# Cross-attention of 16 sequences: a prologue reordered, its work moved among the first heads, and values six heads behind

## Chip, core and metric

One NeuronCore of a Trainium2 chip runs the whole kernel. The metric is the device time of one execution in microseconds (us).

## What is computed

```python
mu = jnp.mean(input, axis=(1, 2), keepdims=True)
var = jnp.var(input, axis=(1, 2), keepdims=True)
xn = (input - mu) * jax.lax.rsqrt(var + EPS)
xn = xn * gamma[None, :, None] + beta[None, :, None]
q = jnp.einsum('oc,ncs->nos', Wq, xn) + bq[None, :, None]
kv = jnp.einsum('od,nds->nos', Wkv, context) + bkv[None, :, None]
q = q.reshape(n, h, c, s).transpose(0, 1, 3, 2)
kv = kv.reshape(n, 2 * h, c, -1).transpose(0, 1, 3, 2)
k, v = (kv[:, :h], kv[:, h:])
att = jax.nn.softmax(jnp.einsum('nhqc,nhkc->nhqk', q * scale, k * scale), axis=-1)
y = jnp.einsum('nhqk,nhkc->nhqc', att, v)
y = y.transpose(0, 1, 3, 2).reshape(n, h * c, s)
return input + jnp.einsum('co,nos->ncs', Wo, y) + bo[None, :, None]
```

There are 16 sequences of 64 channels and 256 positions, 8 heads of 64 channels, and a context of the same shape as x. All is float32.

## The kernel before

Everything is done per sequence n and head h. The products of weights are made once: A = Wq transposed times Wk for each head (`products_a`, split into a high part in a format that TensorE takes at full speed, `a_hi`, and the rest, `a_lo`), and B = Wv times Wo for each head (`b_sb`, then scaled and split into `b_w`). So a head needs these steps:

- t: A applied to the normalised x, two heads a turn (L383, L384), in a PSUM bank. ScalarE copies the high part (`t_a`, L519), VectorE subtracts it from the bank for the low part (`t_b`, L722). Then the bank is free. In the steady stretch there is one bank, `ps_t`.
- first maxima: one coarse product of `t_a` and the context (L420) into `ps_max` (two banks, one a head); VectorE takes the negative maximum of each row (L738). The maxima of a sequence are transposed on TensorE (L464) into `ps_m`, copied by ScalarE (L545) and brought by a DMA as one more row into `t_b`, so that the scores come out with the maximum taken off.
- scores: `c_seq` with `t_a` and `t_b` (L401, L402) into `ps_sc` (two banks). ScalarE makes the exponential twice, in fp16 (`p_hi`, L527, four buffers) and in fp32 (`p_full`, L529, two buffers), and GpSimd subtracts them (`p_lo`, L609). `p_full` of head h therefore waits for `p_lo` of head h - 2. For the last heads VectorE makes every second `p_lo` (`LO_ON_VECTOR`).
- u: B applied to the context, two products (kt = 0, 1) for each sequence into `ps_m` (L454, L455), split by ScalarE (`u_hi`, L538) and VectorE (`u_lo`, L776).
- values: `p_hi` and `p_lo` times `u_hi` and `u_lo` (L361 to L363), 24 matmuls a pair of heads into `ps_z`, with the sum of the exponentials as one more column. VectorE takes the reciprocal and scales (L733, L745, `z_n`).
- the eight heads are added in three steps (`z_4` on GpSimd L617, `z_2` on VectorE L756, `z_1` on GpSimd L623), transposed on TensorE (L432, "y") into `ps_m`, added to the residual x (L768, `x_res`) and stored.

`ps_m` is one bank for u, the transposed maxima and y, so these follow each other.

Each engine runs the same function `step(n, h)` in order and meets the others at semaphores. `at(n, h, shift)` says which head lies `shift` steps on: t is made 14 heads ahead (`T_AHEAD`), the first maxima 12 ahead (`MAX_AHEAD`), the values of a pair of heads 4 behind. In a step TensorE does: values, t, scores, maxima, y, u, transposed maxima. y lies at h = 1, u at h = 3 and 7, the transposed maxima at h = 5. `run` starts at n = -3, writes sequences up to 1 out, loops over pairs of sequences 2 to 11, and writes the rest out again.

The prologue before the steps loads x in two layouts (`x_res` for the statistics and the residual, `x_raw` for the products), the context and the weights, makes A, the statistics of all sequences (L665, then means across partitions by TensorE, L320 and L324), and the scale and shift of x (L681 to L689). x is then normalised and split: for sequences 0 and 1 on VectorE and ScalarE straight into `x_seq`, for the others by GpSimd (`xn`, L584), ScalarE (high, L499) and VectorE (low, L648) into `x_all`, from which a DMA brings each sequence into `x_seq`. The context is split by GpSimd in four chunks (L571, L573). A bound for u (`tops` over the flat context, L698, and over B, L707) gives the scale of B (L711 to L716), and GpSimd splits B (L590 to L594). GpSimd adds the output bias to all of `x_res` in one instruction (L603).

## Time and profile before

| | us |
|---|---|
| median of 3 runs | 246.66 (246.32 to 248.56) |
| the profiled execution | 246.8 |
| its span in the profile | 245.0 |
| busy: TensorE matmuls | 214.4 |
| busy: VectorE | 214.4 |
| busy: ScalarE | 194.2 |
| busy: GpSimd | 195.6 |

The span is what the profile covers; 1.8 us of the profiled execution lie outside it. Busy times are sums over the span, and a stretch in which an engine is busy all the time can lie beside one in which it waits. In the profile PE is TensorE (PEld its weight loads, which overlap the matmuls), DVE is VectorE, ACT is ScalarE, POOL is GpSimd, SP the engine that issues the DMAs.

### The profile page before, as it was taken

The numbers are of one execution on the slowest core, as the hardware profiler recorded it, in microseconds if no ns is written. First come the engines' busy times: TensorE is split into PE (matmuls) and PEld (weight loads), VectorE is DVE, ScalarE is ACT, GpSimd is POOL, SyncE is SP. The second block draws the span as 40 slices with busy tenths as digits, with TensorE's granted clock in tenths as the row PEclk, the third lists the DMA queues.
The fourth block names the chain that finished last, engine by engine and source line by source line (L and its number), as shares of the span: only waits on it lengthen the run. The fifth ranks groups of instructions, "written<-read, shape, count | busy, mean of one in ns | idle before, by whom it ended". The sixth has DMA issues, their size and how long they took to land.

```text
span 245.0 us, 8138 instructions
## 1 busy us (share of the span) xinstructions
PE 214.4 (87%) x2746; PEld 199.0 (81%) x2746; DVE 214.4 (87%) x447; ACT 194.2 (79%) x391; POOL 195.6 (80%) x188
## 2 busy tenths in 40 slices
PE   0663597799889999999999999999999999998962
PEld 0563476699779999999999999999999999996851
DVE  3288998999997999999999999999999999997684
ACT  2244324999788999999999999999999999999860
POOL 3036995877998998989898989898989999998580
PEclk9999999999999999999999999999999999999996
DMA  6999601121032121212121212121212121010000
GB/s 141 219 284 211 141 3 55 32 58 36 2 89 64 36 68 35 64 33 64 33 64 33 64 33 64 33 64 33 64 33 64 37 64 36 13 33 17 13 0 23
DMA packets 13412, 15.08 MB, mean 62 GB/s; under 512 B 2064, under 2 KB 11920, under 8 KB 13200
## 3 DMA queue, kind: packets, MB, share of 16 engines
q1 hardware_dynamic: 13072, 14.16, 21.9%
q10 hardware_dynamic: 320, 0.66, 1.2%
q8 instruction: 11, 0.18, 0.3%
q14 instruction: 9, 0.07, 0.1%
HBM read 5.90 MB, written 1.05 MB: 28 GB/s over the span
## 4 chain that ended last, share of the span: by engine, by line
PE 64%; DVE 11%; POOL 9%; issue 5%; DMA 4%; ACT 4%; SPq 1%; POOLq 0%
PE ps_max L420 10%; PE ps_sc L401 10%; PE ps_sc L402 10%; POOL p_lo L609 8%; PE ps_t L383 6%; PE ps_z L361 6%; PE ps_z L363 5%; PE ps_z L362 5%; PE ps_t L384 5%; DMA x_res<-x_tiles 4%; PE ps_m L455 3%; PE ps_m L454 3%; DVE neg_max L738 1%; DVE x_seq L648 1%; ACT p_full L529 1%
## 5 line engine op out<-in xcount | busy, mean ns | idle before, releaser
L609 POOL TENSOR_TENSOR p_lo<-p_full,p_hi 128x512 f16<-128x512 f32 x122 | 142.8, 1189 | 23.1 <-ACT p_full L529 23.0
L738 DVE TENSOR_REDUCE neg_max<-ps_max 128x2 f32<-128x512 f32 x128 | 84.4, 663 | 0.0
L529 ACT ACTIVATE p_full<-ps_sc 128x512 f32<-128x512 f32 x128 | 78.4, 613 | 0.5 <-POOL p_lo L609 0.5
L527 ACT ACTIVATE p_hi<-ps_sc 128x512 f16<-128x512 f32 x128 | 77.0, 602 | 1.9 <-PE ps_sc L402 1.8
L401 PE MATMUL ps_sc<-t_a,c_seq 128*128 128x256 f32 x256 | 67.8, 286 | 0.2 <-ACT p_full L529 0.2
L402 PE MATMUL ps_sc<-t_b,c_seq 65*128 65x256 f32 x256 | 67.4, 284 | 0.0
L361 PEld LDWEIGHTS ps_z<-u_hi,p_hi 128*128 128x128 f16 x512 | 46.4, 97 | 13.2 <-issue 10.8
L361 PE MATMUL ps_z<-u_hi,p_hi 128*128 128x65 f16 x512 | 52.9, 194 | 3.2 <-DVE p_lo L783 2.4
L362 PE MATMUL ps_z<-u_lo,p_hi 128*128 128x64 f16 x512 | 52.7, 192 | 0.0
L363 PE MATMUL ps_z<-u_hi,p_lo 128*128 128x65 f16 x512 | 52.7, 193 | 0.0
L519 ACT ACTIVATE t_a<-ps_t 128x512 fp32r<-128x512 f32 x60 | 35.9, 598 | 18.5 <-PE ps_t L384 17.5
L401 PEld LDWEIGHTS ps_sc<-t_a,c_seq 128*128 128x128 f32 x256 | 48.5, 189 | 0.4 <-ACT p_full L529 0.4
L402 PEld LDWEIGHTS ps_sc<-t_b,c_seq 65*128 65x128 f32 x256 | 48.6, 190 | 0.0
L722 DVE TENSOR_TENSOR t_b<-ps_t,t_a 64x512 fp32r<-64x512 f32 x60 | 40.9, 682 | 7.7 <-ACT t_a L519 5.8
L362 PEld LDWEIGHTS ps_z<-u_lo,p_hi 128*128 128x128 f16 x512 | 46.5, 98 | 0.3
L363 PEld LDWEIGHTS ps_z<-u_hi,p_lo 128*128 128x128 f16 x512 | 46.6, 97 | 0.0
L420 PE MATMUL ps_max<-c_max,t_a 128*128 128x256 f32 x224 | 45.1, 282 | 0.0
L383 PE MATMUL ps_t<-x_seq,a_hi 128*128 128x256 f32 x120 | 36.9, 329 | 6.0 <-ACT x_seq L497 3.9
L420 PEld LDWEIGHTS ps_max<-c_max,t_a 128*128 128x128 f32 x224 | 35.1, 191 | 0.0
L384 PE MATMUL ps_t<-x_seq,a_lo 128*128 128x256 f32 x120 | 31.7, 286 | 0.0
L383 PEld LDWEIGHTS ps_t<-x_seq,a_hi 128*128 128x128 f32 x120 | 23.5, 196 | 7.3 <-ACT x_seq L497 3.9
L776 DVE TENSOR_TENSOR u_lo<-ps_m,u_hi 128x512 f16<-128x512 f32 x32 | 22.0, 687 | 5.4 <-ACT u_hi L538 5.4
(101 smaller groups left out, 311.3 us busy)
## 6 DMA issues: line engine op xcount, KB each, us to landing
ctx_raw<-ctx SPq DMA_DIRECT2D x8, 256.0 KB, 17.0
c_seq<-c_all SPq DMA_DIRECT2D x16, 128.0 KB, 2.0
x_seq<-x_all SPq DMA_DIRECT2D x14, 128.0 KB, 2.0
c_max<-c_all SPq DMA_DIRECT2D x14, 128.0 KB, 2.0
x_res<-x_tiles SPq DMA_DIRECT2D x4, 256.0 KB, 7.2
z_n<-ctx_flat SPq DMA_DIRECT2D x1, 1024.0 KB, 14.7
c_seq<-c_all SPq DMA_DIRECT2D x16, 64.0 KB, 2.0
out<-x_res SPq DMA_DIRECT2D x16, 64.0 KB, 1.7
```

The source lines that it names most:

```text
L361: mm(ps_z[:, bank, z0:z0 + Z_W], p_hi[:, buf, kt, qs], u_h, start=(kt == 0), stop=False)
L362: mm(ps_z[:, bank, z0:z0 + C], p_hi[:, buf, kt, qs], u_l, start=False, stop=False)
L363: last = mm(ps_z[:, bank, z0:z0 + Z_W], p_lo[:, buf, kt, qs], u_h, start=False, stop=(kt == KT - 1))
L383: mm(bank[:, k * S:(k + 1) * S], a_hi[:, head + k, :], x_seq[:, q, 0, :], start=True, stop=False)
L384: last = mm(bank[:, k * S:(k + 1) * S], a_lo[:, head + k, :], x_seq[:, q, 1, :], start=False, stop=True)
L401: mm(ps_sc[:, bank, kt * S:(kt + 1) * S], c_seq[:, par, 0, keys], t_a[:, par, head, :], start=True, stop=False)
L402: last = mm(ps_sc[:, bank, kt * S:(kt + 1) * S], c_seq[0:C + 1, par, 1, keys], t_b[0:C + 1, par, head, :], start=False, stop=True)
L420: last = mm(ps_max[:, bank, qt * S:(qt + 1) * S], t_a[:, q, head, qt * P:(qt + 1) * P], c_m, start=True, stop=True)
L527: nc.scalar.activation(p_hi[:, buf, :, :].rearrange("p t s -> p (t s)"), scores, ACT.Exp).then_inc(act_phi, 1)
L529: nc.scalar.activation(p_full[:, head % 2, :], scores, ACT.Exp).then_inc(act_p, 1)
L609: nc.gpsimd.tensor_tensor(p_lo[:, buf, :, :].rearrange("p t s -> p (t s)"), p_full[:, head % 2, :], p_hi[:, buf, :, :].rearrange("p t s -> ...
L738: nc.vector.tensor_reduce(neg_max[:, (par + dn) % 2, head, :], ps_max[:, head % 2, :].rearrange("p (t s) -> p t s", t=KT), X, ALU.max, neg ...
```

## The change

- **Steps.** `run` starts at n = -1, and nothing is looped. Up to step (1, 1) tables say which t turn, which first maxima, which `t_b`, which u and which transposed maxima belong to a step. Of the t turns, the first seven use four banks (`ps_t`, `ps_z` twice, `ps_sc`). The first maxima of sequence 0 follow each other in steps (-1, 1) to (-1, 6), and its four `t_b` come after them at (-1, 7).
- **Prologue.** The DMAs are issued in another order, wk and w on the SP queue; the last two context pieces are loaded from steps (-1, 1) and (-1, 2). TensorE runs 16 products of constants as soon as these are there, and 4 more before t (`keep_warm`); `products_a` and `products_b` go around the statistics' products. ScalarE makes x of sequences 0 and 1 by one activation with scale and bias (`scaled`), and the high parts of the context. The rsqrt refinement is one VectorE instruction shorter. The flat maximum of the context, the bound, the scale and the split of B (now ScalarE and VectorE) and u of sequence 0 come in steps (0, 0) to (0, 5).
- **x for later sequences.** For sequences 2 to 5 GpSimd normalises, for 6 to 15 ScalarE does, one sequence a step (m - 6, 4), with the high part at (m - 6, 6). The low part of every sequence from 2 on is GpSimd's; for m from 6 on at step (m - 5, 3). The low parts of the later context pieces are GpSimd's at (0, 2), (1, 2) and (4, 2), each behind a wait for its own `p_lo`. The output bias is added to `x_res` in four chunks, at (1, 6), (5, 6), (9, 6) and (13, 6).
- **Buffers and order.** `p_hi` and `p_lo` have 8 buffers instead of 4; `p_full` keeps 2. The values of a pair lie 6 steps behind instead of 4. From step (1, 2) on y is at h = 2, the transposed maxima at h = 4, u at h = 5 and 7, and the first u product waits for `act_mt` of its own sequence. `z_4` moves to h = 5, `z_2` to h = 7, `z_1` to h = 0 of the next sequence.

```diff
-T_EARLY = 6
-T_AHEAD, MAX_AHEAD, AV_BEHIND = 14, 12, 3
+T_EARLY = 7
+T_AHEAD, MAX_AHEAD, AV_BEHIND = 14, 12, 5
+P_BUFS = 8
+POOL_XN = 6
+WARM_MEAN, WARM_T = 16, 4
+BO_COL = 300
 CHUNK = 4
-PIECES = ((0, 1), (1, 2)) + tuple((n, n + 2) for n in range(2, N, 2))
+C_PIECES = ((0, 2), (2, 4), (4, 8), (8, 12), (12, 16))
+X_LOADS = ((0, 2), (2, 4), (4, 8), (8, 16))
...
-        p_hi = sb("p_hi", [P, 4, KT, S], fp16)
-        wq_bq = p_hi[0:C].rearrange("p b t s -> p (b t s)").bitcast(fp32).rearrange("p (h c) -> p h c", h=H)
-        p_lo = sb("p_lo", [P, 4, KT, S], fp16)
+        p_hi = sb("p_hi", [P, P_BUFS, KT, S], fp16)
+        wq_bq = p_hi[0:C, 0:4].rearrange("p b t s -> p (b t s)").bitcast(fp32).rearrange("p (h c) -> p h c", h=H)
+        p_lo = sb("p_lo", [P, P_BUFS, KT, S], fp16)
...
+        def t_bank_free(turn):
+
+            return 0 if turn < 4 else turn - 3 if turn < T_EARLY else turn - 2 if turn == T_EARLY else turn
+
+        T_FIRST = {(-1, 0): ((0, 0),), (-1, 1): ((0, 2),), (-1, 2): ((0, 4),), (-1, 4): ((0, 6),), (-1, 7): ((1, 0),),
+                   (0, 0): ((1, 2),), (0, 2): ((1, 4),), (0, 3): ((1, 6),), (0, 5): ((2, 0),), (0, 6): ((2, 2),),
+                   (1, 0): ((2, 4),), (1, 1): ((2, 6),)}
+        MAX_FIRST = {(-1, 1): ((0, 0),), (-1, 2): ((0, 1),), (-1, 3): ((0, 2), (0, 3)), (-1, 5): ((0, 4), (0, 5)),
+                     (-1, 6): ((0, 6), (0, 7)), (-1, 7): ((1, 0),), (0, 0): ((1, 1),), (0, 1): ((1, 2),), (0, 2): ((1, 3),),
+                     (0, 3): ((1, 4), (1, 5)), (0, 4): ((1, 6),), (0, 5): ((1, 7),), (0, 6): ((2, 0),), (0, 7): ((2, 1), (2, 2)),
+                     (1, 0): ((2, 3),), (1, 1): ((2, 4), (2, 5))}
+        T_LO_FIRST = {(-1, 7): ((0, 0), (0, 2), (0, 4), (0, 6)), (0, 0): ((1, 0),), (0, 1): ((1, 2),), (0, 2): ((1, 4),),
+                      (0, 3): ((1, 6),), (0, 5): ((2, 0),), (0, 6): ((2, 2),), (1, 0): ((2, 4),), (1, 1): ((2, 6),)}
+        U_FIRST = {(0, 4): (0, 0), (0, 5): (0, 1), (0, 7): (1, 0), (1, 1): (1, 1)}
+        MT_FIRST = {(-1, 7): 0, (0, 6): 1}
+
+        def ahead(first, n, h, shift, every):
+
+            if (n, h) < (1, 2):
+                return first.get((n, h), ())
+            e = at(n, h, shift) if h % every == 0 else None
+            return (e,) if e else ()
...
+        def u_step(n, h):
+
+            if (n, h) < (1, 2):
+                return U_FIRST.get((n, h))
+            return (n + 1, h // 7) if h in (5, 7) and n + 1 < N else None
+
+        def mt_at(n, h):
+
+            if n < 1:
+                return MT_FIRST.get((n, h))
+            return n + 1 if h == 4 and n + 1 < N else None
+
+        XN_AT = {(m - 6, 4): m for m in range(POOL_XN, N)}
+        X_HIGH_AT = {(-1, 4): 2, (-1, 5): 3, (-1, 6): 4, (0, 0): 5} | {(m - 6, 6): m for m in range(POOL_XN, N)}
+        X_LOW_AT = {(m - 5, 3): m for m in range(POOL_XN, N)}
+        X_STAGE_AT = {(0, 0): 2} | {(m - 3, 5): m for m in range(3, N)}
+        NEG_MAX_AT = {(-1, 7): 0, (0, 7): 1} | {(m - 1, 6): m for m in range(2, N)}
+        LOAD_C_AT = {(-1, 1): 3, (-1, 2): 4}
+        C_HIGH_AT = {(-1, 3): 1, (0, 1): 2, (0, 7): 3, (3, 3): 4}
+        C_LOW_AT = {(0, 2): 2, (1, 2): 3, (4, 2): 4}
+        XB_AT = {(c * CHUNK + 1, 6): c for c in range(N // CHUNK)}
+
+        def run(step):
+
+            for n in range(-1, N + 2):
                 for h in range(H):
-                    step(n, n // 2, n % 2, h)
-            with eng.Fori(FIRST // 2, (LAST + 1) // 2) as pair:
...
             for c in range(N // CHUNK):
                 sp.dma_start(x_res[:, chunk(c), :], x_tiles_in[:, chunk(c), :]).then_inc(dma_xt[c], 16)
-            sp.dma_start(x_raw[:, chunk(0), :], x_in[:, chunk(0), :]).then_inc(dma_x[0], 16)
+            sp.dma_start(wk_sb, wk_in).then_inc(dma_qk, 16)
+            load_x(sp, 0)
             load_ctx(sp, 0)
+            sp.dma_start(w_sb[0:C, 0:W_BO], w_in[:, 0:W_BO]).then_inc(dma_w, 16)
+            load_x(sp, 1)
+            load_ctx(sp, 1)
+            load_x(sp, 2)
             sp.dma_start(ctx_spread, ctx_flat_in).then_inc(dma_flat, 16)
-            load_ctx(sp, 1)
-            sp.dma_start(x_raw[:, CHUNK:N, :], x_in[:, CHUNK:N, :]).then_inc(dma_x[1], 16)
-            for c in range(2, N // CHUNK):
-                load_ctx(sp, c)
+            load_ctx(sp, 2)
+            load_x(sp, 3)
 
             x_from, x_to, c_from = x_all[:].bitcast(fp32), x_seq[:].bitcast(fp32), c_all[:].bitcast(fp32)
             c_to, c_max_to, rows_from = c_seq[:].bitcast(fp32), c_max[:].bitcast(fp32), neg_max_rows[:].bitcast(fp32)
...
+                if (m := X_STAGE_AT.get((n, h))):
+                    sp.wait_ge(pe_t, (m - 1) * PAIRS)
+                    sp.wait_ge(pe_s1, (m - 1) * H)
+                    sp.wait_ge(act_xhi, m + 1)
+                    sp.wait_ge(pool_xlo, m + 1 - DIRECT)
+                    c_ready(sp, m)
...
+            def keep_warm(count):
+                for _ in range(count):
+                    mm(ps_z[:, 0, 0:P], ident[:], mean_w[:], start=True, stop=True)
...
             pe.wait_ge(pool_const, 4)
+            keep_warm(WARM_MEAN)
             pe.wait_ge(dve_stats, N)
             for a in range(2):
                 last = mm(ps_m[:, a * N:(a + 1) * N], mean_w[:], stats[:, :, 1 + 3 * a], start=True, stop=True)
             last.then_inc(pe_mean, 1)
+            pe.wait_ge(dma_qk, 16 * 2)
+            products_a(0)
 
             pe.wait_ge(dve_q, 1)
             mm(ps_m[:, 64:64 + 2 * N], mean_w[:], dev2[:].rearrange("p n a -> p (n a)"), start=True, stop=True).then_inc(pe_var, 1)
-
...
+            products_a(1)
+            pe.wait_ge(dma_w, 16)
+            pe.wait_ge(dma_w_tail, 32)
+            pe.wait_ge(dve_var, 1)
+            products_b()
+            keep_warm(WARM_T)
+
...
+                if (n, h) == (0, 1):
+                    pe.wait_ge(dve_tops, 2)
+                    pe.wait_ge(act_mt, 1)
+                    nc.tensor.transpose(ps_m[0:1, 0:P], tops[:, 0:1], ident[:])
+                    nc.tensor.transpose(ps_m[0:1, P:2 * P], tops[:, 1:2], ident[:]).then_inc(pe_tops, 1)
+                if (n, h) == (0, 2):
+                    pe.wait_ge(dve_bound, 1)
+                    mm(ps_m[:, S:S + 1], ones_row[:], u_bound[:], start=True, stop=True).then_inc(pe_bound, 1)
+
                 if e := u_step(n, h):
...
+                    if kt == 0:
+                        pe.wait_ge(dma_cseq[q], 32 * (m // 2 + 1))
+                        pe.wait_ge(act_mt, m + 1)
+                        if m == 0:
+                            pe.wait_ge(act_bhi, 1)
+                            pe.wait_ge(dve_blo, 1)
+                            pe.wait_ge(dve_ones, 3)
                     else:
...
+                if n >= 0 and (m := mt_at(n, h)) is not None:
+                    transpose_max(m)
+
+            def transpose_max(m):
+                pe.wait_ge(dve_max, (m + 1) * H)
+                if m == 0:
+                    pe.wait_ge(dve_bo, 1)
+                elif m < 3:
+                    pe.wait_ge(dve_ulo, 2 * m)
+                else:
+                    pe.wait_ge(dve_y, m - 2)
+                nc.tensor.transpose(ps_m[0:H * KT, 0:P], neg_max[:, m % 2, :, :].rearrange("p h t -> p (h t)"),
+                                    ident[:]).then_inc(pe_mt, 1)
...
+            def scaled(to, m, signal):
+                act.wait_ge(dma_x[next(g for g, (_, end) in enumerate(X_LOADS) if m < end)], 16)
+                slots = to.shape[1]
+                nc.scalar.activation(to, x_raw[:, m:m + 1, :].broadcast_to([C, slots, S]), ACT.Identity, bias=xn_shift[0:C, m:m + 1],
+                                     scale=xn_scale[0:C, m:m + 1]).then_inc(signal, 1)
...
+                if n >= 0 and (m := mt_at(n, h)) is not None:
+                    transpose_out(m)
+
+                if (n, h) == (-1, 0):
+                    scaled(x_seq[0:C, 1, :, :], 1, act_xhi)
+                if (n, h) == (-1, 1):
+                    act.wait_ge(pe_bw, 1)
+                    nc.scalar.activation(b_sb, ps_sc[:, 1, :], ACT.Copy).then_inc(act_b, 1)
+                if (n, h) == (-1, 2):
+                    act.wait_ge(act_table, 1)
+                    nc.scalar.activation(warm[:], ones_row[:, 0:1], ACT.Exp).then_inc(act_table, 1)
+                if (n, h) == (0, 3):
+                    act.wait_ge(dve_uscale, 1)
+                    nc.scalar.activation(b_w[:, 0, :], b_sb, ACT.Copy, scale=u_scale[:]).then_inc(act_bhi, 1)
+                if (m := XN_AT.get((n, h))):
+                    scaled(xn[:, m:m + 1, :], m, act_xn)
+                if (m := X_HIGH_AT.get((n, h))):
+                    if m < POOL_XN:
+                        act.wait_ge(pool_xn, m + 1)
+                    else:
+                        act.wait_ge(act_xn, m + 1 - POOL_XN)
+                    nc.scalar.activation(x_all[0:C, m, :], xn[:, m, :], ACT.Copy).then_inc(act_xhi, 1)
+                if (c := C_HIGH_AT.get((n, h))):
...
+            def x_low(m):
+                pool.wait_ge(act_xhi, m + 1)
+                if m < POOL_XN:
+                    pool.wait_ge(pool_xn, m + 1)
+                else:
+                    pool.wait_ge(act_xn, m + 1 - POOL_XN)
+                nc.gpsimd.tensor_tensor(x_all[C:P, m, :], xn[:, m, :], x_all[0:C, m, :].bitcast(fp32), ALU.subtract).then_inc(pool_xlo, 1)
+                pool.wait_ge(pool_xlo, m + 1 - DIRECT)
+
+            pool.wait_ge(dve_scale, 1)
+            for m in range(4):
+                normalise(m)
+            pool.wait_ge(dve_xlo, 1)
+            pool.wait_ge(pool_xn, 4)
+            c_low(1)
+            x_low(2)
+            x_low(3)
+            normalise(4)
+            normalise(5)
+            pool.wait_ge(pool_xn, 6)
+            x_low(4)
+            x_low(5)
...
+                if (m := X_LOW_AT.get((n, h))):
+                    pool.wait_ge(pool_plo, n * H + h)
+                    x_low(m)
+                if (c := C_LOW_AT.get((n, h))):
+                    pool.wait_ge(pool_plo, n * H + h)
+                    c_low(c)
+                if (c := XB_AT.get((n, h))) is not None:
                     pool.wait_ge(dve_bo, 1)
-                    nc.gpsimd.tensor_scalar(x_res[:], x_res[:], 1.0, bo2[:], ALU.mult, ALU.add).then_inc(pool_xb, 1)
-                if (e := at(n, h, 0)) and not (isinstance(e[0], int) and e[0] * H + e[2] in LO_ON_VECTOR):
-                    m, dn, head = e
-                    buf = head % 4
-                    need(pool, act_p, m * H + head + 1)
-                    need(pool, pe_av, m * H + head - 3)
+                    nc.gpsimd.tensor_scalar(x_res[:, chunk(c), :], x_res[:, chunk(c), :], 1.0, bo2[:], ALU.mult, ALU.add).then_inc(pool_xb, 1)
+                if (e := at(n, h, 0)) and e[0] * H + e[1] not in LO_ON_VECTOR:
+                    m, head = e
+                    buf = head % P_BUFS
...
+            chain(nc.vector.scalar_tensor_tensor(out=y2[:], in0=y1[:], scalar=-3.0, in1=y0[:], op0=ALU.add, op1=ALU.mult))
+            dve.wait_ge(dma_w_tail, 32)
+            chain(nc.vector.tensor_scalar(xn_scale[0:C], y2[0:C], w_sb[0:C, W_GAMMA:W_GAMMA + 1], -0.5, ALU.mult, ALU.mult))
             chain(nc.vector.tensor_tensor(xn_shift[0:C], mu[0:C], xn_scale[0:C], ALU.mult))
...
+            a_low(0)
             x_low(0)
-            x_low(1)
-
-            dve.wait_ge(dma_flat, 16)
-            nc.vector.tensor_reduce(tops[:, 0:1], ctx_spread, X, ALU.max, apply_absolute_value=True).then_inc(dve_tops, 1)
-            dve.wait_ge(pe_bw, 1)
...
+            def step(n, h):
+
+                if (n, h) == (-1, 5):
+                    x_low(1)
+                    dve.wait_ge(pe_bw, 1)
+                    nc.vector.tensor_tensor(bo2[:], ps_m[:, BO_COL:BO_COL + 1], w_sb[:, W_BO:W_BO + 1], ALU.add).then_inc(dve_bo, 1)
+                if (n, h) == (0, 0):
+                    dve.wait_ge(dma_flat, 16)
+                    nc.vector.tensor_reduce(tops[:, 0:1], ctx_spread, X, ALU.max, apply_absolute_value=True).then_inc(dve_tops, 1)
                     dve.wait_ge(act_b, 1)
                     nc.vector.tensor_reduce(tops[:, 1:2], b_sb, X, ALU.max, apply_absolute_value=True).then_inc(dve_tops, 1)
-
-                if peeled_step(n, h, -1, 0):
+                if (n, h) == (0, 2):
                     dve.wait_ge(pe_tops, 1)
                     chain(nc.vector.tensor_reduce(top[:], ps_m[0:1, 0:2 * P].rearrange("p (a q) -> p a q", a=2), X, ALU.max))
                     nc.vector.tensor_tensor(u_bound[:], top[:, 0:1], top[:, 1:2], ALU.mult).then_inc(dve_bound, 1)
-                if peeled_step(n, h, -1, 3):
+                if (n, h) == (0, 3):
                     dve.wait_ge(pe_bound, 1)
...
```

## Rows read from the trace of the kernel before

**Rows 1.** Timeline, TensorE: start us, us, engine, line, operation, tiles

```profile
43.87 0.28 PE L401 MATMUL ps_sc<-t_a,c_seq 128*128 128x256 f32 x1
...
74.57 0.28 PE L401 MATMUL ps_sc<-t_a,c_seq 128*128 128x256 f32 x1
```

**Rows 2.** Stretches: us, then busy us of PE, PEld, DVE, ACT, POOL; granted clock, DMA

```profile
220.00:232.00 12.00, 10.62 (x167) 9.13 (x165) 8.91 (x20) 10.62 (x22) 8.51 (x9) 1.00 0.05 14
...
173.60:197.90 24.30, 24.30 (x340) 22.98 (x337) 22.63 (x49) 22.70 (x48) 21.97 (x21) 1.00 0.17 50
...
197.90:222.00 24.10, 24.10 (x347) 22.93 (x344) 22.63 (x49) 22.61 (x47) 22.39 (x21) 1.00 0.13 37
```

**Rows 3.** Timeline of the prologue, all engines

```profile
8.50 3.78 PE L309 MATMUL ps_max<-p_full,p_hi 64*128 64x128 f32 x16 [8.50 <-DMA p_full<-wk]
...
12.32 0.87 DVE L665 BATCH_NORM_STATS2 stats<-x_res 128x6 f32<-128x128 f32 x4 [1.91 <-DMA x_res<-x_tiles]
...
13.34 1.00 PE L320 MATMUL ps_m<-stats,mean_w 128*128 128x16 f32 x4 [1.07 <-DVE stats L665]
...
17.55 2.34 POOL L573 TENSOR_TENSOR c_all<-ctx_raw,c_all 64x1024 fp32r<-64x1024 f32 x1
...
18.07 1.86 DVE L682 TENSOR_TENSOR y<-y 128x16 f32<-128x16 f32 x1
...
21.05 0.23 DVE L689 TENSOR_SCALAR xn_shift<-xn_shift,w_sb 64x16 f32<-64x16 f32 x1
```

**Rows 4.** Groups by form: shapes, count | busy us, mean ns | idle before, releaser

```profile
L609 POOL TENSOR_TENSOR p_lo<-p_full,p_hi 128x512 f16<-128x512 f32 x122 | 142.8, 1189 | 23.1 <-ACT p_full L529 23.0
...
L738 DVE TENSOR_REDUCE neg_max<-ps_max 128x2 f32<-128x512 f32 x128 | 84.4, 663 | 0.0
...
L722 DVE TENSOR_TENSOR t_b<-ps_t,t_a 64x512 fp32r<-64x512 f32 x60 | 40.9, 682 | 7.7 <-ACT t_a L519 5.8
...
L508 ACT ACT_TABLE_LOAD x1 | 1.3, 1283 | 0.0
...
L698 DVE TENSOR_REDUCE tops<-z_n 128x1 f32<-128x2048 f32 x1 | 2.3, 2286 | 0.0
...
L617 POOL TENSOR_TENSOR z<-z_n 128x512 f32<-128x512 f32 x15 | 19.7, 1312 | 0.0
...
L573 POOL TENSOR_TENSOR c_all<-ctx_raw,c_all 64x1024 fp32r<-64x1024 f32 x4 | 9.5, 2374 | 0.3
...
L594 POOL TENSOR_TENSOR b_w<-p_full,b_w 64x512 fp32r<-64x512 f32 x1 | 1.3, 1273 | 0.1
```

**Rows 5.** DMA issues: count, KB each, median us to landing

```profile
t_b<-neg_max_rows SPq DMA_DIRECT2D x16, 8.0 KB, 1.8
```

**Rows 6.** Timeline of TensorE's weight loads, before and behind a change of pace

```profile
42.52 0.33 PEld L455 LDWEIGHTS ps_m<-b_w,c_seq 128*128 128x128 f32 x1
...
43.40 0.19 PEld L384 LDWEIGHTS ps_t<-x_seq,a_lo 128*128 128x128 f32 x1
```

**Rows 7.** Timeline of heads 4 and 5 of sequence 13, ScalarE and TensorE

```profile
211.04 0.60 ACT L519 ACTIVATE t_a<-ps_t 128x512 fp32r<-128x512 f32 x1
...
211.45 0.19 PEld L401 LDWEIGHTS ps_sc<-t_a,c_seq 128*128 128x128 f32 x1
...
211.54 0.59 ACT L527 ACTIVATE p_hi<-ps_sc 128x512 f16<-128x512 f32 x1
...
212.02 0.60 ACT L529 ACTIVATE p_full<-ps_sc 128x512 f32<-128x512 f32 x1
...
212.19 0.09 PEld L464 LDWEIGHTS ps_m<-ident,neg_max 128*16 128x16 f32 x1
...
213.45 0.25 ACT L545 ACTIVATE neg_max_rows<-ps_m 16x128 fp32r<-16x128 f32 x1
```

**Rows 8.** Timeline of ScalarE, tail: first exponentials

```profile
222.66 0.60 ACT L527 ACTIVATE p_hi<-ps_sc 128x512 f16<-128x512 f32 x1 [0.18 <-PE ps_sc L402]
...
236.41 0.59 ACT L527 ACTIVATE p_hi<-ps_sc 128x512 f16<-128x512 f32 x1
```

565 lines of the change are left out of this document (232 added, 333 removed).

## Prediction

> **What bounds the kernel now.** I read the busy time by stretches first, then the timeline of one pair of heads, the prologue's timeline, and the groups by form. Positions (n, h) are sequence and head; the engines' queues are written out in these steps. From the second pair of sequence 2 (first scores at 74.57 us) [rows 1] TensorE is busy without a break: 24.30 of 24.30 us, two sequences [rows 2]. That is about 12.1 us a sequence, and there only TensorE's own work and waits put in its way count. VectorE (22.63), ScalarE (22.70) and GpSimd (21.97 of 24.30) follow closely [rows 2], so none of them has more than 1.2 us a sequence to give. Before it lie 43.87 us in which no score is made [rows 1], then 30.7 us for two sequences and one pair, which at 12.1 a sequence would be about 27. After 220 us TensorE has gaps again: 10.62 of 12.00 [rows 2]. The change can win in the front and in the tail, and can only lose in the middle.
>
> **Up to the scale of x (gain about 4.3 us).** The last chunk of x_res lands at 12.32 [rows 3], with three weight loads of the other queue beside it. The change leaves only wq and two small tails beside it, some 0.4 MB less; with 1.5 to 2 MB moved by then I take 10.1, with bounds of 9 and 12.3. Then: statistics to 11.0; mean products 1.15 (13.34 and 1.00, less the statistics' end at 13.19) [rows 3]; four small VectorE steps 0.9, to 13.0. products_a(0) now lies ahead of the variance product: half of 3.78 [rows 3] ends at 14.05, so it costs 1 us if the array is slow, nothing at double speed. Variance product and square root with their hops 1.3, to 15.35. The chain of VectorE steps to xn_shift ends at 21.28 now, with one step of 1.86 us in it, which ends as GpSimd's c_all split (17.55 plus 2.34) does [rows 3]. That split is gone from there, the chain is one step shorter, and some 1.65 us remain: 17.0 against 21.28. Without the wait each such step costs 0.2.
>
> **From there to the first scores.** VectorE sets the pace, by instruction, with start-to-start times of [rows 4] (0.60 for a group of mean 0.66 to 0.68, since neighbours overlap; a_low is like t_b, but alone): a_low(0) 1.35; x_low(0) 0.45; the low part of two ctx sequences 0.7; a_low(1) 1.35; eight first maxima 4.8; x_low(1) and bo2 0.6; gaps 0.4; four t_b 2.4. That is 12.05. Four of these have both inputs in SBUF while GpSimd now works through eleven instructions of its own (0.55 to 1.3 us each). The one-step wait above is the nearest row: I add 1.25, bounds 0 and 4. First scores: 30.3 instead of 43.87. The Trainium skill, "SBUF — State Buffer", section Who interferes with whom, says that such a VectorE instruction and a GpSimd instruction that reads SBUF exclude each other for a whole instruction. The row agrees: 16 columns took 1.86 us. By that rule alone the 1.25 could be up to four whole GpSimd instructions, about 3 us, and the sum 1.8 worse. The maxima's row goes by ScalarE and a DMA of 1.8 us [rows 5] beside the t_b steps and ends at the same time; it is issued behind the last bulk loads on the SP queue, and if they end late scores wait with it. ScalarE's x split, b copy and Exp table load fit in its gaps here. keep_warm and the reordered products touch nothing behind VectorE: a load of 128 columns took 0.33 us until 42.5 and 0.19 from 43.4, the lower and the upper of the two clock levels [rows 6] at a granted clock of 1.00, and even at the lower one TensorE has spare time in this stretch. I value the warming at 0, bounds minus 1.5 and plus 0.5.
>
> **Sequences 0 and 1 give a good half of it back.** What the old prologue had done (two more t turns, the flat ctx maximum of 2.29 us [rows 4], the bound, b_w, all u) now lies among the heads of sequence 0. VectorE there: six t_b 3.6, ten maxima 6.0, flat and b maxima 2.9, bound and scale 1.6, b low 1.1, three u_lo 2.0, one z 0.5: 17.7. u of both halves and the first values form one file of hops (b low, u product, u_hi, u_lo, second u, first values, next t), during which VectorE idles some 3. So sequence 0 takes 20.7 and (1,0) starts at 51.0. In sequence 1 the first pair waits on one t bank twice, 4.6 instead of 2.8; GpSimd has there 8 p_lo of 1.15, z_4 1.3, x_low, a c_low of 2.4 and one x_res chunk of 0.7, 14.5 in all, of which 1 us comes through. (2,0) starts at 65.8 and the pair behind it at 68.4, against 74.57 [rows 1]: gain 6.2.
>
> **Steady stretch: one new wait.** The transposition of the maxima moves from h = 5 to h = 4, the first u product from h = 3 to h = 5, and that u product now waits for ScalarE's copy of the transposed row (ps_m is one bank). Between the two TensorE has one head: 0.74 (211.45 to 212.19) [rows 7]. In the pair shown, the transposition would start at 211.45, the head end and u be due at 212.30. ScalarE's order is t_a 211.04, p_hi 211.54, p_full 212.02, and the copy comes next, at 212.50, and takes 0.25 [rows 7]. u waits until 212.80: 0.50. Were t_a out of ScalarE's way it would be 0.2. Behind u on TensorE wait the values and the next t, so it is a loss of the bounding engine. I take 0.30, nearer to the lower, as the ends of matmuls that fix this pair are modelled and the whole wait is one difference between two engines' rows: for n = 2 to 14, the last counted half because the tail has room, 12.5 times 0.30 is 3.8, bounds 0 and 6.3. The row of maxima itself is ready 0.1 us late at worst, hidden in the same wait. y at h = 2 has 2.7 us to be read: nothing. The change unrolls the loop of sequences 2 to 11. In the part that is unrolled already, two sequences take 24.10 without a gap where the looped ones take 24.30 [rows 2]; ten sequences would give 1.0, and as the second stretch ends where t work thins out I take 0.4.
>
> **GpSimd and ScalarE in the steady stretch.** x_low comes to GpSimd for one sequence per sequence. From 2.37 at 1024 columns and 1.27 at 512 [rows 4] it is 0.72 at 256, and two self-waits make it 0.9. So 8 times 1.145 plus 1.31, 0.46 and 0.9 is 11.8 of 12.1 (before 10.9). x_res chunks at n = 5 and 9 and c_low at n = 4 come on top. p_full still has two buffers, so the lag that eight p_hi buffers allow for the values is not allowed for the exponentials: p_full(h) waits for p_lo(h-2), with 1.2 us to spare. The 2.5 of n = 4 exceed it once: 0.9, bounds 0 and 3. ScalarE gets two copies of 256 columns, 0.3 each, on 11.35: hidden while the wait above leaves it time. The normalisation becomes an Identity with scale and bias between Exps; sixty Copy between Exps needed no table load, so I take none. The Trainium skill, "ScalarE: Activation LUTs", section Table sets, has identity in every set; no run here shows it.
>
> **Tail.** From (14,4) on no t or maxima are left. The first exponentials run from 222.66 to 236.41 [rows 8], 13.75 for eleven heads, while GpSimd waits for ScalarE and TensorE for p_lo. With the values two heads later this can be 2.1 to 2.2 a pair: gain 1.7, bounds 0 and 3. The last values wait for p_lo of the last head as now, and the extra pair of values (0.75) fits in that wait.
>
> **Sum.** 245.0 - 6.2 + 3.8 - 0.4 + 0.9 - 1.7 = 241.4 of span. The profiled execution took 246.8 with 1.8 outside the span, 0.14 from the median 246.66. So 243.2 us, 1.4% faster. A measurement of this kernel tells about 1% (2.5 us) from no change.
>
> **Rivals.** (a) The new wait doesn't show and sequence 0 is limited by VectorE's work alone: minus 3.8 and minus 1.5, 238. For it: the hops are hand-estimated from gaps. Against: the order of the queues. (b) Slower: GpSimd becomes the bound in sequences 1 to 10. It decides from the point where x_low costs 1.2, which is what the 512-column form takes [rows 4], for then every insertion passes through p_full to TensorE: 4.8 for two c_low, 1.9 for three chunks, and 0.15 a sequence, some 8 in place of 1.9, so 249.5. For it: 97% load already by my sum. Against: the new wait gives GpSimd time. (c) The front isn't shortened by as much, because x_res lands at 12.3 and the ctx loads hold the row of maxima: 3.3 less gain, 246.5. (d) The change does not do what it says for Identity: a table load of 1.28 us [rows 4] twice per sequence, ten times, 25.6 more, 269.
>
> **How the numbers follow.** Forecast 0.45 (own range 240.5 to 246), (a) 0.25, (b) 0.15, (c) 0.12, (d) 0.03. Under 244.2 lie 0.6 of the forecast and all of (a): with a sliver of (c), 0.53. Within 1% (to 249.1) lie the rest of the forecast, most of (c) and a third of (b): 0.33. Slower 0.14. The range goes from 237, just under (a), to 249.5, through most of (b).
>
> **What would show it.** First scores near 30 and the second pair of sequence 2 near 68 in the timeline; TensorE's u product waiting for ScalarE's neg_max_rows about 14 times, 0.3 each; GpSimd near 97% between; no table load after the third. Wrong would make it: TensorE without gaps from (1,2) on (then a), or ScalarE's p_full waiting for p_lo in most sequences (then b).

## Result and the profile after

The changed kernel takes 256.79 us (median of 4 runs, 255.07 to 258.45) against 246.49 (4 runs, 245.86 to 248.56) for the kernel before: a ratio of 1.040, 95% interval 1.030 to 1.051. It is 4% slower, where 1.4% faster was forecast, and lies above the range. The profiled execution took 258.45 us with a span of 256.7, 11.7 above the span before. Each kernel has executions in a faster and in a slower state: medians here are of all its runs, ratios and their intervals of the faster ones alone.

Page of the changed kernel: busy time by engine, and in 40 slices TensorE's busy share and granted clock.

```profile
PE 227.0 (88%) x2786; PEld 207.9 (81%) x2786; DVE 202.5 (79%) x439; ACT 203.1 (79%) x412; POOL 196.4 (77%) x190
...
PE   7796776789989999799999999999999999998762
...
PEclk9959586599999999799999999999999999999896
```

TensorE's busy time has grown by 12.6 us with nothing more to compute beyond the 20 warming products; a good part of it is time at the lower of TensorE's two clock levels (slices with 5 to 8 in the last line; the mean granted clock is 0.93, before 0.99). No engine is full over the span, so the loss has to be found by place. Where the first exponential (p_hi of head 0) of a sequence starts, from ScalarE's timeline of both kernels, tells that:

| sequence | before | changed | length before | length changed |
|---|---|---|---|---|
| 0 | 45.06 | 31.09 | 13.04 | 23.46 |
| 1 | 58.10 | 54.55 | 13.30 | 14.86 |
| 2 | 71.40 | 69.41 | 13.23 | 13.49 |
| 3 | 84.63 | 82.90 | 12.09 | 13.11 |
| 4 | 96.72 | 96.01 | 12.11 | 15.72 |
| 5 | 108.83 | 111.73 | 12.12 | 12.71 |
| 6 | 120.95 | 124.44 | 12.08 | 12.99 |
| 7 to 13 | 133.03 | 137.43 | 12.03 to 12.12 | 12.70 to 12.74 |
| 14 | 217.59 | 226.44 | 10.64 | 10.97 |
| last head | 236.41 | 247.22 | | |

The front wins 14.0 us at the first exponential and 3.1 at the second pair of sequence 2; the steady stretch loses 0.6 in every sequence, 3 more in sequence 4, and 0.3 to 0.8 more in sequences 2, 3 and 6; the tail loses 2.9 (30.26 from (14,0) to the end against 27.41).

Timeline of the changed kernel at the places of [rows 1, 3], VectorE and TensorE:

```profile
8.43 0.87 DVE L723 BATCH_NORM_STATS2 stats<-x_res 128x6 f32<-128x128 f32 x4 [0.20 <-DMA x_res<-x_tiles]
...
13.49 0.23 DVE L744 TENSOR_SCALAR xn_shift<-xn_shift,w_sb 64x16 f32<-64x16 f32 x1
...
29.99 0.42 PE L430 MATMUL ps_sc<-t_a,c_seq 128*128 128x256 f32 x1
...
71.43 0.28 PE L430 MATMUL ps_sc<-t_a,c_seq 128*128 128x256 f32 x1
```

The scale of x is ready at 13.7 instead of 21.3, and first scores come at 30.0, as forecast. That the two agree is partly luck, as the part on the prediction shows. The second pair of sequence 2 comes at 71.43 and not at 68.4.

Stretches, columns as in [rows 2]: two sequences while x_low stands on GpSimd, and two after the last x_low.

```profile
163.20:188.70 25.50, 24.83 (x335) 23.05 (x334) 22.58 (x49) 23.28 (x49) 24.29 (x24) 1.00 0.17 50
188.70:214.20 25.50, 24.83 (x335) 23.04 (x334) 22.00 (x49) 22.74 (x47) 22.33 (x21) 1.00 0.17 49
```

The groups that answer to [rows 4], with the two new ones of the steady stretch:

```profile
L673 POOL TENSOR_TENSOR p_lo<-p_full,p_hi 128x512 f16<-128x512 f32 x122 | 144.4, 1194 | 28.7 <-ACT p_full L570 26.8
...
L640 POOL TENSOR_TENSOR x_all<-xn,x_all 64x256 fp32r<-64x256 f32 x14 | 10.2, 729 | 5.3 <-ACT p_full L570 4.3
...
L521 ACT ACTIVATE xn<-x_raw,xn_shift,xn_scale 64x256 f32<-64x256 f32 x10 | 5.9, 585 | 0.0
```

x_low takes 0.73, as forecast. TensorE now stands idle for 0.67 us of two sequences, where it had no gap [rows 2]. GpSimd has 2 us less to do in the second stretch, and it takes exactly as long: in this kernel GpSimd doesn't set the pace. What does, the pair of heads 4 and 5 shows (sequence 9; [rows 7] has it before):

```profile
168.02 0.60 ACT L559 ACTIVATE t_a<-ps_t 128x512 fp32r<-128x512 f32 x1 [0.38 <-PE ps_t L411]
...
168.44 0.09 PEld L500 LDWEIGHTS ps_m<-ident,neg_max 128*16 128x16 f32 x1
...
168.99 0.60 ACT L570 ACTIVATE p_full<-ps_sc 128x512 f32<-128x512 f32 x1
...
169.01 0.31 PEld L451 LDWEIGHTS ps_max<-c_max,t_a 128*128 128x128 f32 x2
...
169.47 0.25 ACT L548 ACTIVATE neg_max_rows<-ps_m 16x128 fp32r<-16x128 f32 x1
...
169.83 0.19 PEld L486 LDWEIGHTS ps_m<-b_w,c_seq 128*128 128x128 f32 x1 [0.51 <-issue]
```

The maxima are transposed at 168.44, ScalarE copies the row behind p_full, at 169.47, and the u product, which could start at 169.32, starts at 169.83. The waits of the whole span (the waiting group, what it waited for: total, times, longest):

```profile
PEld ps_m L486 <- issue: 11.7, 15, 2.0
...
PE ps_m L486 <- ACT neg_max_rows L548: 7.2, 14, 1.8
...
PE ps_m L463 <- POOL z L687: 4.4, 4, 2.0
...
ACT p_full L570 <- POOL p_lo L673: 2.3, 4, 1.3
```

### The profile page after: what moved, and what is told of

Its sections match the earlier page's. It is cut to its first block, busy times and chain, and to the rows that moved or that the text cites. A ratio compares the mean times of both kernels' runs of the same rounds, so it can differ in the third digit from the quotient of the medians.

```text
span 256.7 us, 7528 instructions
## 1 busy us (share of the span) xinstructions
PE 227.0 (88%) x2786; PEld 207.9 (81%) x2786; DVE 202.5 (79%) x439; ACT 203.1 (79%) x412; POOL 196.4 (77%) x190
## 4 chain that ended last, share of the span: by engine, by line
POOL 51%; issue 23%; PE 11%; DVE 8%; ACT 3%; DMA 2%; POOLq 1%; SPq 0%; ACTq 0%
POOL p_lo L673 37%; POOL z L681 7%; DVE neg_max L795 3%; POOL z L687 3%; POOL x_all L640 3%; DMA x_res<-x_tiles 2%; PE ps_t L410 1%; POOL c_all L630 1%; DVE t_b L780 1%; PE ps_max L451 1%; PE ps_t L411 1%; DVE tops L761 1%; PE ps_max L337 1%; POOL x_res L667 1%; PE ps_z L332 1%
## 5 line engine op out<-in xcount | busy, mean ns | idle before, releaser
L673 POOL TENSOR_TENSOR p_lo<-p_full,p_hi 128x512 f16<-128x512 f32 x122 | 144.4, 1194 | 28.7 <-ACT p_full L570 26.8
L430 PE MATMUL ps_sc<-t_a,c_seq 128*128 128x256 f32 x256 | 72.3, 303 | 0.1
L431 PE MATMUL ps_sc<-t_b,c_seq 65*128 65x256 f32 x256 | 69.2, 290 | 0.0
L390 PE MATMUL ps_z<-u_hi,p_hi 128*128 128x65 f16 x512 | 55.2, 198 | 1.4 <-DVE u_lo L829 1.4
L391 PE MATMUL ps_z<-u_lo,p_hi 128*128 128x64 f16 x512 | 54.6, 195 | 0.0
L392 PE MATMUL ps_z<-u_hi,p_lo 128*128 128x65 f16 x512 | 54.5, 196 | 0.0
L430 PEld LDWEIGHTS ps_sc<-t_a,c_seq 128*128 128x128 f32 x256 | 51.4, 201 | 0.6 <-issue 0.2
L431 PEld LDWEIGHTS ps_sc<-t_b,c_seq 65*128 65x128 f32 x256 | 50.6, 198 | 0.0
L391 PEld LDWEIGHTS ps_z<-u_lo,p_hi 128*128 128x128 f16 x512 | 47.8, 100 | 0.0
L801 DVE TENSOR_TENSOR z_n<-ps_z,inv_sum 128x256 f32<-128x256 f32 x64 | 26.0, 407 | 0.3
```

The source lines that it names most:

```text
L390: mm(ps_z[:, bank, z0:z0 + Z_W], p_hi[:, buf, kt, qs], u_h, start=(kt == 0), stop=False)
L391: mm(ps_z[:, bank, z0:z0 + C], p_hi[:, buf, kt, qs], u_l, start=False, stop=False)
L392: last = mm(ps_z[:, bank, z0:z0 + Z_W], p_lo[:, buf, kt, qs], u_h, start=False, stop=(kt == KT - 1))
L430: mm(ps_sc[:, bank, kt * S:(kt + 1) * S], c_seq[:, q, 0, keys], t_a[:, q, head, :], start=True, stop=False)
L431: last = mm(ps_sc[:, bank, kt * S:(kt + 1) * S], c_seq[0:C + 1, q, 1, keys], t_b[0:C + 1, q, head, :], start=False, stop=True)
L673: nc.gpsimd.tensor_tensor(p_lo[:, buf, :, :].rearrange("p t s -> p (t s)"), p_full[:, head % 2, :], p_hi[:, buf, :, :].rearrange("p t s -> ...
```

## Experiments

All are edits of the changed kernel; in the cuts of code "..." stands for what is left out. "Before" beside each ran on the same chip as the edit, median 246.28 to 246.88, but not all edits ran on one chip: compare their ratios, not their times.

**e1: the row copy behind p_hi.**

```
                     nc.scalar.activation(p_hi[...], scores, ACT.Exp).then_inc(act_phi, 1)
+                    if n >= 1 and (r := mt_at(n, h)) is not None:
+                        transpose_out(r)
                     lo_done(act, m, head - 2)
                     nc.scalar.activation(p_full[...], scores, ACT.Exp).then_inc(act_p, 1)
...
-                if n >= 0 and (m := mt_at(n, h)) is not None:
+                if n == 0 and (m := mt_at(n, h)) is not None:
                     transpose_out(m)
```

> Edit: from sequence 1 on ScalarE copies the transposed maxima between p_hi and p_full of head 4, not behind p_full. Theory 1 (TensorE is the bound, and the longer time of a sequence is the first u product's wait for this copy): the copy ends some 0.48 us earlier, the wait of the u line falls from 7.2 + 11.7 us to under half, and the time falls by 12 to 14 times 0.4 to 0.5, to 250 to 252 us. Theory 2 (GpSimd is the bound since it took the low parts of x; the u product only waits in time that would be idle anyway): no more than 1 us, 256.

Measured: 252.41 us, ratio 1.019 (1.010 to 1.029). ScalarE's timeline, and from the list of waits the one that is left:

```profile
166.51 0.59 ACT L568 ACTIVATE p_hi<-ps_sc 128x512 f16<-128x512 f32 x1
166.99 0.25 ACT L548 ACTIVATE neg_max_rows<-ps_m 16x128 fp32r<-16x128 f32 x1
167.14 0.57 ACT L572 ACTIVATE p_full<-ps_sc 128x512 f32<-128x512 f32 x1
```

```profile
PE ps_m L486 <- ACT neg_max_rows L548: 0.6, 2, 0.3
```

The wait falls from 7.2 to 0.6 us and a sequence from 12.71 to 12.31, although its first exponential came 2.8 later by a slower prologue. Theory 1 holds, for 0.4 of the 0.6 a sequence; the time lies just above its 250 to 252.

**e2: the old order of the steps.** Only av_at, u_step, mt_at and the steps of y, z_4, z_2 and z_1 differ:

```
+            if (n, h) == (1, 4):
+                return ((0, 6), (1, 0))
+            e = at(n, h, -6 if (n, h) < (1, 4) else -4)
...
-            return (n + 1, h // 7) if h in (5, 7) and n + 1 < N else None
+            return (n + 1, h // 7) if h in (5 if n < 2 else 3, 7) and n + 1 < N else None
```

> Edit: from (1,4) on the old order of the steps: values four heads behind the scores (two pairs of values in one step to catch up), y at h = 1, z_4 / z_2 / z_1 at h = 3, 5, 6, u products at h = 3 and 7, transposition of the maxima at h = 5. New prologue, low parts of x on GpSimd, eight p buffers and unrolled steps stay. Theory 1 (the order makes the wait): a sequence falls back from 12.7 to 12.1 us, and the tail to that of before (no wait of y for z_1): minus 7 and minus 3, 246 to 248 us. Theory 2 (GpSimd): a sequence stays near 12.6 and only the tail gains, 253.

Measured: 257.81 us, ratio 1.044 (1.033 to 1.054). A miss of both: the tail is mended (28 us from (14,0)), but a sequence takes 13.0 up to 9 (13.5 with an x_res chunk), and 12.08 from 11 on, where x_low has ended. Timeline of e2, GpSimd in sequence 7 and TensorE's values:

```profile
144.22 0.73 POOL L653 TENSOR_TENSOR x_all<-xn,x_all 64x256 fp32r<-64x256 f32 x1
145.03 1.17 POOL L686 TENSOR_TENSOR p_lo<-p_full,p_hi 128x512 f16<-128x512 f32 x1
146.15 1.27 POOL L694 TENSOR_TENSOR z<-z_n 128x512 f32<-128x512 f32 x1
147.39 1.16 POOL L686 TENSOR_TENSOR p_lo<-p_full,p_hi 128x512 f16<-128x512 f32 x1
...
149.98 0.10 PEld L398 LDWEIGHTS ps_z<-u_hi,p_hi 128*128 128x128 f16 x1 [0.73 <-issue]
```

And from its list of waits:

```profile
PE ps_z L398 <- POOL p_lo L686: 8.0, 19, 2.3
```

With values four heads behind it is they that wait for p_lo, not p_full. Six heads behind, they don't. So in the changed order x_low is hidden, and in this one it isn't. The edit also moved z_4 to h = 3, into the step of x_low, where the kernel before had no x_low and the changed one has no z_4: e2 brings in a pairing that neither of them has.

**e3: no warming** (both counts 0).

> Edit: keep_warm issues nothing (both counts 0). In the changed kernel these products run from 1.8 to 7.7 us and the array is at its upper level only from about 9 to 12.9. Theory: VectorE and the transfers pace the prologue, so the time stays within 0.5 us and first scores at 30 us. Rival: the weights' products are on the path and take double, first scores 1 to 2 us later, 258.

Measured: 259.11 us, ratio 1.047 (1.037 to 1.057), which overlaps the changed kernel's interval. First exponential 32.89 against 31.09, (1,0) 55.54 against 54.55. The first a_hi copy starts at 12.24; in the kernels with the same 16 products it starts at 11.16 (changed), 12.35 (e1) and 13.43 (e7). The clock tells them apart. Each half of products_a takes 1.16 us in the changed kernel and 2.07 in e3, and xn_shift is ready 4.4 us after the last statistics against 6.05. Ten of the twelve profiles with 16 products have the 4.4 to 4.6. In e1 and e7 the granted clock fell before products_a (0.58 and 0.76 between 10 and 11 us), and there it took 5.6 and 5.9. So where the clock stays up the first warming is worth about 1.6 us up to the scale of x. What of it reaches the end isn't settled.

**e4: x_low on VectorE, changed order.**

```
+                if (m := X_LOW_DVE.get((n, h))):
+                    dve.wait_ge(act_xhi, m + 1)
+                    dve.wait_ge(act_xn, m + 1 - POOL_XN)
+                    nc.vector.tensor_tensor(x_all[C:P, m, :], xn[:, m, :], x_all[0:C, m, :].bitcast(fp32), ALU.subtract).then_inc(dve_xlo, 1)
```

> Edit: from sequence 6 on the low part of x is again computed by VectorE, one sequence at a time (0.3 us there for 0.72 to 0.9 on GpSimd). Theory 1: GpSimd is not the bound of the steady stretch, so within 1 us of the changed kernel, 256. Theory 2 (GpSimd is the bound): about 0.5 us for each of ten sequences, 251 to 252.

Measured: 257.55 us, ratio 1.042 (1.032 to 1.053), 12.72 a sequence as before it. GpSimd's load isn't the bound in this order.

**e5: e2 and e4 together.**

> Edit: e2 and e4 together: old order of the steps from (1,4) on, and the low part of x from sequence 6 on by VectorE. In e2 a sequence took 13.0 us while GpSimd had x_low in it and 12.08 after the last x_low; in e4 it took 12.7 with and without. Theory: order (0.6) and x_low on GpSimd (0.9) each suffice to set the pace, so either alone gives nothing and both together give 12.1 a sequence: 251 us. Rival: what stretches e2's sequences up to 10 is the Identity or the extra copy on ScalarE, which stays: 13.0 stays, 257 us.

Measured: 253.19 us, ratio 1.023 (1.013 to 1.033); 12.33 a sequence up to 9, 12.08 after. Either edit alone changes nothing, both together gain 3.6 us. That looks like two costs that hide each other, as the expectation has it, but e13 and e15 read otherwise: in the changed order x_low costs nothing, whether the row copy waits or not. e2 takes 0.6 a sequence away and brings 0.9 in, x_low beside z_4, and moving x_low to VectorE takes that away again. The 0.25 that stay up to 9 are not explained by x_low on GpSimd: with it there, but in another step, e13 keeps only 0.1.

**e6: ctx splits in sequence 0.**

```
-        C_HIGH_AT = {(-1, 3): 1, (0, 1): 2, (0, 7): 3, (3, 3): 4}
-        C_LOW_AT = {(0, 2): 2, (1, 2): 3, (4, 2): 4}
+        C_HIGH_AT = {(-1, 3): 1, (0, 1): 2, (0, 4): 3, (0, 5): 4}
+        C_LOW_AT = {(0, 2): 2, (0, 5): 3, (0, 6): 4}
```

> Edit: the changed kernel with the split of the ctx sequences 4 to 7 into high and low parts moved from steps (0,7)/(1,2) to (0,4)/(0,5), and that of 12 to 15 from (3,3)/(4,2) to (0,5)/(0,6), where ScalarE and GpSimd stand idle for 3 to 5 us. Theory 1 (the 2.4 us GpSimd instruction goes straight through p_full to TensorE): sequence 4 falls from 15.7 to 12.7 and sequence 1 by 1, 252.5 to 254 us. Rival (the stretch of sequence 4 is a clock fall of its own or the order of the steps): 256.5.

Measured: 254.10 us, ratio 1.032 (1.027 to 1.037). Sequence 4 takes 12.73 instead of 15.72, and sequence 0 nothing more. The chain in the changed kernel, where the split was:

```profile
99.95 2.39 POOL L630 TENSOR_TENSOR c_all<-ctx_raw,c_all 64x1024 fp32r<-64x1024 f32 x1
...
103.60 0.60 ACT L570 ACTIVATE p_full<-ps_sc 128x512 f32<-128x512 f32 x1 [1.34 <-POOL p_lo L673]
104.09 0.25 ACT L548 ACTIVATE neg_max_rows<-ps_m 16x128 fp32r<-16x128 f32 x1
...
104.49 0.47 PE L486 MATMUL ps_m<-b_w,c_seq 128*128 128x512 f32 x1 [1.81 <-ACT neg_max_rows L548]
```

A part of the stretch behind it, columns as in [rows 2]:

```profile
106.30:108.40 2.10, 2.10 (x14) 2.10 (x12) 0.92 (x2) 1.02 (x3) 2.10 (x3) 0.50 0.00 0
```

GpSimd's 2.4 us hold up p_full, which holds up the row copy, which holds up TensorE's u product for 1.8 us, 1.3 more than in other sequences. The clock is still granted in full from 104.5 to 105.0; then it falls, and it is 0.50, the lower level, from 105.5 to 108.4, though TensorE is busy all that time. Some 3.3 us at the lower level cost about half of that, and with the 1.3 this is the 3.0 us of sequence 4 (an estimate).

**e7: the u products of sequence 0 behind the scores.**

```
-        U_FIRST = {(0, 4): (0, 0), (0, 5): (0, 1), (0, 7): (1, 0), (1, 1): (1, 1)}
+        U_FIRST = {(0, 5): (0, 0), (0, 6): (0, 1), (0, 7): (1, 0), (1, 1): (1, 1)}
...
+                if (n, h) == (0, 7):
+                    values(0, 0)
```

> Edit: the changed kernel with the two u products of sequence 0 one step later (steps 5 and 6, behind those steps' scores) and its first values behind the scores of (0,7) instead of ahead of those of (0,6). Theory 1 (the chain b_low, u, u_hi, u_lo, u, u_hi, u_lo, values holds back scores that need none of it): the exponential of (1,0) comes 3 to 4 us earlier, at about 51, and most of it stays: 253 us. Rival (VectorE's own work is what fills sequences 0 and 1, or later waits take it back): (2,2) earlier by less than 1 us, 256 us.

The first values now stand behind the scores and maxima of (0,7), not ahead of the scores of (0,6). Measured: 256.98 us, ratio 1.041 (1.034 to 1.049), a miss: 253 was expected. In this profile the first exponential came at 34.94, 3.9 later than in the changed kernel, and (2,0) at 69.19, 0.2 earlier: sequence 0 took 19.37 instead of 23.46. From (0,4) to (0,6) it took 4.6 us instead of 11.3, from (0,6) to (1,0) 6.9 instead of 4.3. Not all of the 4.1 is the edit's: e1, which differs from the changed kernel only later, also started late (33.92) and took 22.04. Where starts are nearly alike the edit gives 1.3 to 1.4 (21.86 in e9 against 23.20 in e6, 21.23 in e8 against 22.65 in e5). The median shows none of it: in sixteen profiles the first exponential comes between 30.6 and 34.9.

**e8: e2, e4, e6 and e7 together.**

> Edit: e2, e4, e6 and e7 together (new prologue and eight p buffers kept; old order from (1,4) on; low part of x on VectorE; ctx splits in sequence 0; u products of sequence 0 behind the scores). Theory: first scores 30, (1,0) at 51, (2,0) at 65 to 66, 12.1 a sequence without the step at 4, and the tail of before: 239 to 241 us, below both kernels. Rival (some of the four gains are the same time): 244 to 247.

Measured: 249.31 us, ratio 1.014 (1.008 to 1.019), a miss: 8 us above the 239 to 241 expected. (1,0) at 52.5, but sequence 1 takes 15.88 and sequence 2 14.20: the switch to the old order comes with two pairs of values in one step, (1,4), and in sequence 2 the u product then waits 1.2 us for VectorE's read of y. That the switch belongs elsewhere was the conclusion for e9.

**e9: the changed order kept.** e1, e6 and e7, and:

```
-        XB_AT = {(c * CHUNK + 1, 6): c for c in range(N // CHUNK)}
+        XB_AT = {(0, 7): 0, (1, 0): 1, (1, 1): 2, (1, 2): 3}
...
-                if h == 2 and n >= 2:
+                if h == 3 and n >= 2:
...
+            if (n, h) == (14, 4):
+                return ((13, 6), (14, 0))
+            e = at(n, h, -AV_BEHIND - 1 if (n, h) < (14, 4) else -AV_BEHIND + 1)
```

> Edit: the changed kernel's order of the steps kept, with e1 (row copy behind p_hi), e6 (ctx splits in sequence 0), e7 (u products of sequence 0 behind the scores), the transposed sum y at h = 3 where values follow it, the four x_res chunks at (0,7) to (1,2), and values four heads behind from (14,4) on. Theory: 12.2 to 12.3 a sequence from the third on (12.31 in e1, less 0.08 for y), no steps at 4, 5 and 9, sequences 1 and 2 as in e6 less 0.4, the tail of before: span 242 to 244, 244 to 246 us, level with or just below the kernel before. Rival (GpSimd with x_low becomes the bound once the order no longer is): 12.6 and more a sequence, 249.

The second pair of lines moves y on TensorE and on VectorE, the last is for the values. Measured: 244.94 us (10 runs) against 246.47, ratio 0.994 (0.990 to 0.998). Two sequences with x_low on GpSimd, and two without:

```profile
129.40:153.70 24.30, 24.30 (x334) 23.03 (x334) 21.96 (x49) 23.44 (x51) 23.41 (x23) 1.00 0.18 52
177.90:202.20 24.30, 24.30 (x334) 23.03 (x333) 22.22 (x49) 22.61 (x48) 22.17 (x21) 1.00 0.17 49
```

12.15 us each, TensorE without a gap, and GpSimd busy for 96% of the first.

**e10: the tail alone** (e9's edit of the values at (14,4), and y at h = 3 from sequence 15 on).

> Edit: the changed kernel, values four heads behind instead of six from (14,4) on (two pairs in that step), and y at h = 3 from sequence 15 on. Theory 1 (the lag of six costs the tail: y waits 1.4 us for z_1, the clock falls in that gap, and one more pair of values stands behind the last exponential): minus 2.5 to 3.5 us, 253.5. Rival (the lag is what my prediction valued at minus 1.7; the tail's loss is z_1 on GpSimd alone): (15,7) comes later than 247.2 or the end no nearer to it than 9.5 us, 256.

Measured: 254.89 us (5 runs), ratio 1.035 (1.030 to 1.040). From (14,0) to the end 29.2 instead of 30.3, before 27.4. A third of the loss.

**e11 and e12: a longer warming** (WARM_MEAN 28), of the changed kernel and of e9.

> Edit: WARM_MEAN 28 instead of 16, so that the products of the warming reach to the statistics' end instead of stopping 1.6 us before it. Theory 1 (whether products_a and the variance product run at the upper level differs from run to run, and is worth 2 to 3 us of the prologue: 11.2 against 12.4 and 13.4 for the first a_hi in the changed kernel, e1 and e7): first a_hi at 11 in every profile, median 1 to 2 us below the changed kernel, 255 us. Rival (it was the arrival of x_res): no difference, 256.8.

> Edit: e9 and e11 together. Theory 1: as e9 less 1 to 2 us, 243 to 245 us. Rival: equal to e9.

Measured: 255.91 us, ratio 1.038 (1.032 to 1.045), and 244.15, ratio 0.993 (0.989 to 0.996): neither differs from its kernel. The first a_hi starts at 12.16 and 12.37, later than the 11.16 of the changed kernel, since the 28 products now outlast the statistics.

**e13: x_low in another step of the old order** (e2 with X_LOW_AT at step 0 of a sequence).

> Edit: e2 with GpSimd's low part of x at step 0 of a sequence instead of step 3, where the old order also has z_4. In e2 a sequence took 13.0 us with x_low and 12.08 without; in e9 GpSimd has the same instructions in 12.15. Theory 1 (no load bound: x_low and z_4 stand behind each other in one step, 2 us, more than the slack between p_full and p_lo of two heads later): a sequence from 5 to 9 takes 12.1 to 12.4, as in e5, 253 us. Theory 2 (GpSimd's load in the old order): 12.9 to 13.0 stays, 257.5 us.

Measured: 252.96 us, ratio 1.024 (1.016 to 1.031). 12.17 to 12.21 a sequence from 5 to 9, but for the 12.6 with an x_res chunk, with x_low on GpSimd and in the old order. The waits of values for p_lo:

```profile
PE ps_z L398 <- POOL p_lo L686: 3.5, 6, 1.8
```

They were 8.0 in 19 times in e2. So e2's 0.9 came from x_low and z_4 in one step, not from GpSimd's load. (Sequence 10, with an x_res chunk, takes 12.40.)

**e14: the sums of sequence 14 earlier** (e12 with z_4 at (15,3), z_2 at (15,5), z_1 at (15,6)).

> Edit: e12 with the sums of sequence 14 two steps earlier (z_4 at (15,3), z_2 at (15,5), z_1 at (15,6)), since its values are now done earlier. In e9 VectorE's p_lo of the last head stands behind z_2, which waits for z_4, and starts 1.9 us after its p_full. Theory: the last p_lo starts 1 to 1.5 us earlier and the end with it, 1 us below e12, 243 us. Rival (z_4 then holds GpSimd's p_lo of heads 3 to 5 back by as much, as in the kernel before): equal to e12, 244.2.

Measured: 242.45 us against 246.88, ratio 0.981 (0.975 to 0.987): faster than both kernels, and than the kernel before by 1.3 to 2.5%. From (14,0) to the end 28.4 us instead of e12's 29.3.

**e15: e9 with x_low on VectorE.**

> Edit: e9 with the low part of x from sequence 6 on by VectorE (as in e4). Theory 1 (GpSimd isn't the bound even at 12.15 us a sequence): within 0.5 us of e9, 245. Theory 2 (it is just the bound): 12.05 a sequence, 1 us below e9. Rival (VectorE is fuller than GpSimd): 12.3 a sequence, 1 to 2 us above e9.

Measured: 244.65 us (10 runs, 240.84 to 246.83) against 246.88, ratio 0.984 (0.979 to 0.990), below e9's 0.994 from another chip: the times alone leave room for a gain of 1%. The pace leaves none: 12.13 to 12.18 a sequence from 3 to 9, in e9 12.14 to 12.18. Once more GpSimd doesn't set it.

## Why the prediction was wrong

The span was to fall by 3.6 and rose by 11.7. As measured its terms are minus 3.1 for the front, plus 7.3 for the order of the steps (with what the loop gives back), plus 3.7 for the insertions and plus 2.9 for the tail; a wait that no term has, 0.7 in sequence 2, comes on top. That makes 11.5. One by one:

**Front, minus 6.2; measured minus 3.1.** The first scores came at 30.0 against 30.3 taken, and that was luck: two errors of 3 us cancel. The scale of x was ready at 13.7, not 17.0: x_res landed by 8.5 (taken 10.1), and products_a ran at the upper level. From there to the scores it took 16.3 us, not 13.3. "VectorE sets the pace" failed: VectorE waited 1.8 us for the first maxima, while TensorE, at a granted clock of 0.50 from 13 us on, made the products of B and then the four warming products ahead of the first t. Timeline of TensorE and VectorE:

```profile
15.54 2.08 PE L332 MATMUL ps_z<-mean_w,ident 128*128 128x128 f32 x8
17.27 0.56 PE L410 MATMUL ps_t<-x_seq,a_hi 128*128 128x256 f32 x1
...
19.98 2.75 DVE L795 TENSOR_REDUCE neg_max<-ps_max 128x2 f32<-128x512 f32 x4 [1.77 <-PE ps_max L451]
```

The inputs of that t were ready at 15.8, when x_low(0) ended, so these four products cost it up to 1.4 us (an estimate; no run leaves out only them). And the last t_b ended 1.7 before the scores, which stand behind a maxima product and a t turn at the lower level. "I value the warming at 0" was wrong at both places.

Rival (d) did not come: there was no table load for Identity. By the Trainium skill, "ScalarE: Activation LUTs", section Table sets, identity is in every set; the trace agrees, ten such activations stand between exponentials without a load.

Sequence 1 took 14.9 (taken 14.8). What failed behind the scores is "during which VectorE idles some 3": sequence 0 took 23.5, not 20.7, with 16.4 us of work for VectorE (17.7 taken) and 7.1 of idle time. The file of hops, work that goes from engine to engine one piece at a time, was named, but priced at the engines' full pace. Timeline of VectorE in that stretch, and the stretch itself:

```profile
39.31 1.70 DVE L774 SCALAR_TENSOR_TENSOR b_w<-b_sb,u_scale,b_w 64x512 fp32r<-64x512 f32 x1
43.13 0.69 DVE L829 TENSOR_TENSOR u_lo<-ps_m,u_hi 128x512 f16<-128x512 f32 x1 [1.51 <-ACT u_hi L577]
...
50.03 0.68 DVE L780 TENSOR_TENSOR t_b<-ps_t,t_a 64x512 fp32r<-64x512 f32 x1 [3.23 <-ACT t_a L559]
```

```profile
41.30:50.30 9.00, 7.58 (x48) 6.68 (x49) 3.25 (x6) 3.88 (x8) 1.89 (x2) 0.50 0.13 39
```

The whole file ran with the array at the lower level, where a t turn takes 0.85 to 1.00 us instead of 0.55 from its start to that of the scores behind it, and VectorE had 3.25 us of work in 9. With the same products behind the scores the granted clock of e7 is 1.00 from 42 to 58 us, and sequence 0 is shorter by 1.3 to 1.4 like with like, 4.1 in e7's own profile. The edit takes away the hops and the lower level together, so how they share the loss isn't shown. The forecast argued that TensorE has spare time at the lower level before the first scores, and didn't ask about the stretch behind them, where others waited for it.

**New wait of the u product, 3.8; measured about 5, and 7.3 with what came beside it (0.61 in each of twelve sequences).** The place, the mechanism and the count (14) were right. The step that failed is "I take 0.30, nearer to the lower". The 0.50 worked out from [rows 7] was the true figure: the trace has 0.51. Taking it out (e1) gives 0.40 a sequence. The rest of the 0.6 the prediction had not seen: y and the transposed maxima now stand ahead of scores instead of ahead of values, and behind each such transposition the first scores matmul is followed by the next after 0.20 us instead of 0.12. With y moved (and the x_res chunks gone from there) e9 has 12.15, 0.16 below e1. Why the smaller value was chosen, "the ends of matmuls are modelled", is an argument for a wider bound, not for a lower value.

**Unrolled loop, minus 0.4.** 12.08 in e2, e5 and e13 from sequence 11 on against 12.08 to 12.12 in the loop: 0.3 at most.

**Insertions on GpSimd, 0.9; measured 3.7.** Sequence 4 alone cost 3.0, sequence 6 0.3 by an x_res chunk, and sequence 3 0.4, which went with the ScalarE half of the ctx split (e6). The prediction took 2.5 less a slack of 1.2. It left out that x_low stands one step behind c_low, that the copy for the u product hangs on p_full, so that its own two mechanisms meet in one pair, and that the clock falls behind the gap. It also had one path only, through p_full. The record shows a second, through z_1 to y. In sequence 1 GpSimd has a c_low, x_low, z_4 and an x_res chunk and works without a break from 59 us on, so z_1 comes late and TensorE's y waits for it:

```profile
72.97 0.33 PE L463 MATMUL ps_m<-ident,z 128*128 128x128 f32 x1 [0.66 <-POOL z L687]
```

In e6, which takes c_low out of (1,2), that wait is gone and sequence 2 takes 13.00 instead of 13.49. In e1 the same wait is 0.62 in sequence 6, behind an x_res chunk, and that sequence takes 0.6 to 0.7 more than its neighbours.

**Tail, minus 1.7; measured plus 2.9.** The term had the wrong sign. It counted what the exponentials gain by values two heads later and not what follows them: z_1 now stands two steps ahead of y, which needs it. TensorE in sequence 15:

```profile
240.81 0.14 PEld L463 LDWEIGHTS ps_m<-ident,z 128*128 128x128 f32 x1 [1.62 <-POOL z L687]
...
242.61 0.32 PEld L430 LDWEIGHTS ps_sc<-t_a,c_seq 128*128 128x128 f32 x1
...
245.47 0.19 PEld L430 LDWEIGHTS ps_sc<-t_a,c_seq 128*128 128x128 f32 x1
```

A gap of 1.6 us for z_1; 0.8 us behind it the clock falls, and from 242 to 245 it is granted at 0.50, with TensorE busy for all of it and weight loads of 0.32 instead of 0.19. e10 and e14 come to 1.0 and 1.9 us less than the changed kernel's 30.3.

**Rivals.** (a) fell with the wait. (b), the slower one, gave the nearest time, 249.5, still 7 us off, and its mechanism is refuted: x_low takes 0.73 us and not 1.2, and off GpSimd it changes nothing (e4, e15). Its price would have been real with values four heads behind and x_low beside z_4 (e2, e13), and it would have gone through TensorE's values, not through p_full. (c) had x_res late; its last chunk landed by 8.5.

Open: what of the warming's 1.6 us reaches the end; the 0.25 a sequence in e5, most of which goes with x_low on VectorE; the last 1 us of the tail against the kernel before, where sequence 14 has both u products two steps later.

## What to carry to other kernels

When a step moves in a queue written by hand, look for the copy or signal that it now waits for, and put that copy as early in its own engine's queue as its input allows: a quarter of a microsecond of work behind an exponential cost 0.4 us in each of twelve sequences. If two rows work out a wait, take what they give. An edit that puts an old order back can bring in a cost of its own: e2 removed 0.6 us a sequence and added 0.9, and its time alone would have cleared the order. Read the waits of such a run before you strike a theory. A total that agrees with the forecast shows nothing until its parts do. And short instructions that an engine must fit in belong in different steps, as far from each other as the order allows.

## What the runs showed of the hardware

TensorE's clock fell after gaps that cost little by themselves, and stayed low with the array busy. After 1.8 us idle it was granted at 0.50 for 2.90 us with TensorE busy for all of them (sequence 4), after 1.6 us idle for 3.0 (tail). In sequence 4 a gap 1.3 us longer than usual cost 3.0.

VectorE and GpSimd held each other up. b_low on VectorE (64x512, both inputs in SBUF) took 1.70 us beside p_lo on GpSimd, and 1.14 in e8, where it met only the last 0.6 us of one; a low part of the same shape with one input in PSUM took 0.68. z_2 (128x256) took 1.36 in the tail of e9, where it started with a p_lo, 0.48 to 0.83 in the other sequences and 0.42 alone; z_4 on GpSimd took 1.72 once, beside a p_lo on VectorE, instead of 1.29. By the Trainium skill, "SBUF — State Buffer", section Who interferes with whom, the two share a port pair that one instruction holds to its end; these times agree.
